# Bonus argument and bonus product of the scan conditions on GpSimd instead of VectorE

## The chip, the cores and the metric

The kernel runs on one core of one Trainium2 chip. The metric is device time in microseconds (us) of one execution; lower is better. Engines are called as in the profile: PE (matmul), PEld (its weight loads), DVE (VectorE), ACT (ScalarE), POOL (GpSimd), SP (the engine that issues most DMAs).

## What is computed

Two transformer layers on x of shape (4, 256, 256): batch 4, 256 tokens, width 256. Each layer is a condition, causal attention with 16 heads of 16, a second condition, and a feed-forward block (an fp8 linear in layer 0, a mixture of 32 experts with top 6 in layer 1). A condition is a bidirectional scan whose k and v are both the side input:

```python
def _bi_wkv(r, k, v, w, u, time_emb):
    tf = sigmoid(sum(time_emb, axis=-1))[:, None, None]
    decay = exp(-exp(w))[None, :] * (0.5 + 0.5 * tf[:, :, 0])
    ek = exp(minimum(k, 30.0)); ekv = ek * v
    # nf, df: forward scans of ekv and ek; nb, db: the backward scans
    euk = exp(minimum(u[None, None, :] + k, 30.0))     # the bonus
    num = nf + nb - ekv + euk * v
    den = df + db - ek + euk
    return sigmoid(r) * (num / maximum(den, 1e-8)) * (0.8 + 0.2 * tf)

x = x + attn0(cond(x, side, side, w0, u0, c))
x = x + ffn0(cond(x, side, side, w1, u1, c))
x = x + attn1(cond(x, side, side, w2, u2, c))
x = x + ffn1(cond(x, side, side, w3, u3, c))
```

There are 4 conditions of 4 batches each, so 16 pairs (condition i, batch b). Since k and v don't depend on x, num / den of a pair can be computed long before its r is known.

## The kernel before

Channels lie on the 128 partitions (NC = 2 chunks), tokens along the free axis. Every engine has its own hand-written program, ordered by semaphores alone; nothing is scheduled by a tool.

**Attention.** `attention(L)` runs for layers L = 0 and 1. It has 16 steps v = 4b + u (batch b, quad of heads u). In step v, PE has made the scores of v+1 (`scores`, L769 and the masks L751); DVE takes their row maxima out of PSUM with two reductions (`maxima`, L1219: first 128 columns by 4 heads, then 256 by 4); PE then makes the turned scores of step v (`turned_scores`, L782, L786, L751), which waits for the maxima of v+1; ACT takes their exponential (`exps`, L463); PE makes the scores of v+2 into the same PSUM tile S, which waits for that exponential; the maxima of v+2 follow. So one turn of the loop is DVE maxima, PE turned scores, ACT exponential, PE scores. Between them PE also does the projections (L701, L732), the output product (L744) and the product with the values (L821).

**Scan work in the gaps.** After the maxima of v+1, DVE's program has scan work of one pair n (`ratio_of` says which). Even u: `bonus_arg` (L1066, two instructions, min(side + u, 30) into eu[.., 1]), `scan_forward` and `scan_backward` of the denominator (L1075, L1078, L1087), `scale_o` of the attention, `denominator` (L1095, L1099). Odd u: in some steps `residual` (L1239), then both scans of the numerator, `numerator` (L1106 the bonus product eu[.., 1] = eu[.., 0] * side, L1110 its sum with the scans), `refine` (L1116, L1118) and either `gate` and `next_input` (L1132, L1141) or `make_ratio` (L1125). 7 pairs are done in attention(0) (v = 0 to 13) and 6 in attention(1) (v = 0 to 11); pairs n = 0, 1 and 9 are done outside of the loops.

**ACT.** In an even step ACT's program is: `spread_decay` (L424), `bonus_exp` (L432, two instructions, waits for `bonus_arg`), in most steps `totals_inverse` (L475, L477), `exps` (L463), and later `inverse` (L439, L441), which waits for `denominator`.

**POOL.** Memsets at the start, a `partition_all_reduce` of the weight maximum (L361) and, after attention(0), one of the input maximum (L365); then nothing until the indirect DMAs of the experts (L374), whose first one waits for step 12 of attention(1).

## Time and profile before

| | |
|---|---|
| median of 3 runs | 635.13 us (633.89 to 639.38) |
| the profiled execution | 637.68 us |
| its span, first to last instruction | 635.8 us |
| mean granted TensorE clock | 0.924 |
| DVE busy | 493.5 us, 78% |
| PE busy | 489.2 us, 77% |
| ACT busy | 336.2 us, 53% |
| POOL busy | 216.5 us, 34% |
| attention(0), attention(1) | about 47 to 163 us, 214 to 345 us |

Times in rows are counted from the first instruction. In a timeline a row is a start, a duration, the engine, the line of the kernel, the operation, what it writes <- reads, and how many instructions the row merges; a bracket at its end is the engine's idle time ahead of it and what ended that. Ends of matmuls are modelled.

### The profile page before, as it was taken

To read this page: it belongs to the slowest core of one execution; us is meant where nothing else is said; L and a number is where in the kernel's file an instruction comes from. 1 tells how busy PE (TensorE), PEld (TensorE's weight loads), DVE (VectorE), ACT (ScalarE), POOL (GpSimd) and SP (SyncE) were. 2 spreads that over 40 slices of the span, in tenths; PEclk is the share of its full clock that TensorE was granted. 3 is DMA by queue.
4 is the path that set the end of the run, shared out by engine and by line. 5 is a ranking of instruction groups with operands and counts; after the bars stand their busy time and mean duration, and the time that the engine had idled before them with its cause. 6 is when DMAs were issued, how large, how long until landed. Compare 5 with 4: busy or idle time off the path is not lost.

```text
span 635.8 us, 13234 instructions
## 1 busy us (share of the span) xinstructions
PE 489.2 (77%) x4916; PEld 402.2 (63%) x4916; DVE 493.5 (78%) x963; ACT 336.2 (53%) x663; POOL 216.5 (34%) x165
## 2 busy tenths in 40 slices
PE   0268889897725598898959659989999999999930
PEld 0147667675514376676746435589999999999930
DVE  2997999999475789999963680379999999999910
ACT  4334565655565155657532521257777777777720
POOL 3000000000000000000007277508888888888881
PEclk9977999999957699999968988999999999999985
DMA  8999910000000000000002173375997869779323
GB/s 296 282 240 234 249 34 3 1 2 2 2 2 0 0 2 1 3 3 2 1 2 104 31 276 113 125 258 161 244 232 195 227 173 247 203 192 253 37 27 66
DMA packets 56720, 71.89 MB, mean 113 GB/s; under 512 B 11777, under 2 KB 45036, under 8 KB 56544
## 3 DMA queue, kind: packets, MB, share of 16 engines
q1 hardware_dynamic: 40272, 57.35, 31.2%
q0 software_dynamic: 16400, 13.87, 11.0%
q8 instruction: 33, 0.54, 0.4%
q14 instruction: 15, 0.12, 0.1%
HBM read 42.09 MB, written 37.04 MB: 124 GB/s over the span
## 4 chain that ended last, share of the span: by engine, by line
DVE 51%; PE 28%; issue 12%; ACT 5%; DMA 2%; POOL 1%; DVEq 1%; POOLq 0%; SPq 0%; ACTq 0%
DVE negmax L1219 9%; PE S L751 4%; DVE both L1087 3%; DVE wgu_s L1477 3%; DVE fwd L1075 3%; PE S L782 3%; DVE xgT L1496 3%; PE PJ L701 3%; DVE sg L1505 3%; PE S L769 3%; PE S L940 3%; DVE ek L1502 3%; DVE hidden_s L1511 3%; DVE wgu_s L1479 2%; PE S L786 2%
## 5 line engine op out<-in xcount | busy, mean ns | idle before, releaser
L999 PE MATMUL S<-xgT,wgu_s 128*128 128x384 f32 x576 | 108.0, 340 | 8.2 <-DVE sg L1505 7.4
L374 POOL DMA_INDIRECT xe_rows<-x_tok,slot_i x48 | 47.7, 994 | 177.6 <-issue 165.8
L999 PEld LDWEIGHTS S<-xgT,wgu_s 128*128 128x128 f32 x576 | 98.8, 188 | 14.6 <-issue 14.6
L385 POOL DMA_INDIRECT out<-sig,y_token x48 | 81.1, 1690 | 36.9 <-ACT sig L655 22.1
L385 POOL DMA_INDIRECT odd_out<-sig,y_token x48 | 81.0, 1688 | 14.7 <-issue 14.4
L463 ACT ACTIVATE prob<-S 128x1536 f32<-128x1536 f32 x32 | 46.4, 1451 | 60.2 <-PE S L751 59.7
L1219 DVE TENSOR_REDUCE negmax<-S 128x4 f32<-128x512 f32 x64 | 58.2, 952 | 16.2 <-PE S L751 16.2
L782 PE MATMUL S<-q_sb,k_sb 32*128 32x128 f32 (+1 forms) x512 | 37.9, 368 | 29.1 <-DVE negmax L1219 29.1
L365 POOL PARTITION_ALL_REDUCE amax_x<-amax_x x1 | 0.4, 375 | 151.5 <-DVE amax_x L1209 151.5
L782 PEld LDWEIGHTS S<-q_sb,k_sb 32*128 32x128 f32 x512 | 24.6, 196 | 38.6 <-DVE negmax L1219 36.9
L1014 PE MATMUL PJ<-wd_s,hidden_s 128*128 128x256 f32 x320 | 43.3, 282 | 1.9 <-ACT sig L655 1.9
L1014 PEld LDWEIGHTS PJ<-wd_s,hidden_s 128*128 128x128 f32 x320 | 41.9, 189 | 2.0 <-issue 2.0
L751 PE MATMUL S<-causal_b,ident_b 128*128 128x128 bf16 x512 | 42.6, 230 | 0.0
L769 PE MATMUL S<-k_sb,q_sb 32*128 32x256 f32 (+1 forms) x512 | 33.2, 377 | 11.3 <-ACT q_sb L497 6.9
L751 PEld LDWEIGHTS S<-causal_b,ident_b 128*128 128x128 bf16 x512 | 31.0, 102 | 16.3 <-issue 12.9
L1075 DVE TENSOR_TENSOR_SCAN fwd<-decay_t,ek 128x512 f32<-128x512 f32 x32 | 38.9, 1215 | 2.9 <-ACT decay_t L424 2.8
L1087 DVE TENSOR_TENSOR_SCAN both<-decay_t,fwd 128x512 f32<-128x512 f32 x32 | 39.2, 1224 | 1.3 <-DVE fwd L1078 0.3
L432 ACT ACTIVATE eu<-eu,neg_ln_q 128x256 f32<-128x256 f32 x32 | 14.5, 499 | 48.5 <-DVE eu L1066 44.7
L1496 DVE TENSOR_TENSOR xgT<-TB,xgT 128x384 fp32r<-128x384 f32 x64 | 32.7, 552 | 2.4 <-ACT xgT L645 1.5
L786 PE MATMUL S<-neg_rows,pick 32*128 32x128 f32 (+1 forms) x512 | 34.5, 341 | 0.0
L663 ACT ACTIVATE hidden_s<-ek 128x384 fp32r<-128x384 f32 x32 | 16.7, 523 | 28.7 <-DVE ek L1502 26.1
L769 PEld LDWEIGHTS S<-k_sb,q_sb 32*128 32x128 f32 x512 | 18.9, 201 | 20.0 <-issue 17.4
(212 smaller groups left out, 1083.3 us busy)
## 6 DMA issues: line engine op xcount, KB each, us to landing
xe_rows<-x8m SPq DMA_DIRECT2D x4, 3468.0 KB, 38.7
ratio<-xe_rows SPq DMA_DIRECT2D x32, 433.5 KB, 3.7
ek<-in_wgu SPq DMA_DIRECT2D x32, 384.0 KB, 4.4
x8m<-in_wd SPq DMA_DIRECT2D x32, 256.0 KB, 4.9
x<-in_x SPq DMA_DIRECT2D x1, 1024.0 KB, 7.0
odd_out<-x8m SPq DMA_DIRECT2D x1, 1024.0 KB, 26.5
out<-side SPq DMA_DIRECT2D x8, 128.0 KB, 5.6
out<-odd_out POOLq DMA_DIRECT2D x1, 1024.0 KB, 8.0
```

The costliest lines, as they stand in the source:

```text
L374: eng.indirect_dma_start(xe_rows, bass.IndirectOffsetOnAxis(slot_i[:, t, k:k + 1], 0), x_tok[:, t, :], None, bounds_check=ROWS - 1, oob_is ...
L385: eng.indirect_dma_start((out, odd_out)[j % 2], bass.IndirectOffsetOnAxis(y_token[:, j, t:t + 1], 0), ye_sb[:, j % 2, t, :], None, bounds_ ...
L751: ins = eng.matmul(S[:, i, lo:lo + P], ident_b[:, :], causal_b[:, turned, :], start=False, stop=lo > 0, skip_group_check=True)
L769: eng.matmul(S[:, i, cols], q_sb[rows, b % 2, u, st * P:(st + 1) * P], k_sb[rows, b % 2, u // 2, 0:P * (st + 1)], start=st == 0, stop=Fals ...
L782: eng.matmul(S[:, i, cols], k_sb[rows, b % 2, u // 2, kt * P:(kt + 1) * P], q_sb[rows, b % 2, u, q_cols], start=kt == 0, stop=False, skip_ ...
L786: eng.matmul(S[:, i, cols], pick[rows, :], neg_rows[rows, v % 2, q_cols], start=False, stop=False, skip_group_check=True)
L999: ins = eng.matmul(S[:, m, 0:CAP], fast(wgu_s[:, j % 2, a, k, m * P:(m + 1) * P]), fast(xgT[:, j % 2, b, k, :]), start=n == 0, stop=n == N ...
L1014: ins = eng.matmul(dst, fast(hidden_s[:, j % 2, h, t * P:(t + 1) * P]), fast(wd_s[:, j % 2, a, part, :]), start=n == 0, stop=n == 4)
L1075: eng.tensor_tensor_scan(flat(fwd[:, kv, :, :]), decay_t[:, buf, 0:NC * T], ek_of(kv, b), 0.0, ALU.mult, ALU.add).then_inc(sem("forward"), 1)
L1087: eng.tensor_tensor_scan(flat(both[:, kv, :, :])[:, ::-1], decay_t[:, buf, NC * T:0:-1], flat(fwd[:, kv, :, :])[:, ::-1], 0.0, ALU.mult, A ...
L1219: ins = eng.tensor_reduce(negmax[:, v % 2, st, :, 0], S[:, :, cols], AX.X, ALU.max, negate=True)
L1496: eng.tensor_tensor(fast(xgT[:, j % 2, LO, k, :]), TB[:, k, 0:CAP], xgT[:, j % 2, HI, k, :], ALU.subtract)\
```

## The change

`bonus_arg` and the bonus product of the 13 pairs that are done inside `attention` leave DVE's program and are written on POOL, in `bonuses(L)`. Each waits for a new semaphore `max_half`, which DVE raises when the first of the two reductions of a step's maxima is done. The bonus product further waits for `bonus_exp`, as it did on DVE. `numerator` on DVE now begins with the wait for `bonus_made`. `bonuses(0)` stands on POOL between the two `partition_all_reduce`, `bonuses(1)` behind the second. The three pairs outside of the loops stay on DVE.

```diff
@@ POOL
             eng.partition_all_reduce(gmax[:, 1:2], amax_w[:, :], P, bass.bass_isa.ReduceOp.max)\
                .then_inc(sem("gmax_w"), 1)
 
+            def bonuses(L):
+                for b in range(B):
+                    for u in range(QUADS):
+                        v = b * QUADS + u
+                        ratio_now = ratio_of(L, b, u)
+                        if ratio_now:
+                            i, bb, n, buf = ratio_now
+                            eng.wait_ge(sem("max_half"), B * QUADS * L + v + 2)
+                            if u % 2 == 0:
+                                eng.wait_ge(sem("num_made"), n - 1)
+                                settle(eng, "pool")
+                                for c in range(NC):
+                                    ins = eng.tensor_scalar(eu[:, buf, 1, c, :], side[:, c, tok(bb)],
+                                                            vec[:, V_U + i * NC + c:V_U + i * NC + c + 1], 30.0,
+                                                            ALU.add, ALU.min)
+                                ins.then_inc(sem("bonus_arg"), 1)
+                            else:
+                                eng.wait_ge(sem("bonus_exp"), n + 1)
+                                settle(eng, "pool")
+                                eng.tensor_tensor(eu[:, buf, 1, :, :], eu[:, buf, 0, :, :], side[:, :, tok(bb)],
+                                                  ALU.mult).then_inc(sem("bonus_made"), 1)
+
+            bonuses(0)
             eng.wait_ge(sem("amax_x"), B)
             eng.partition_all_reduce(amax_x[:, 1, :], amax_x[:, 0, :], P, bass.bass_isa.ReduceOp.max)\
                .then_inc(sem("gmax_x"), 1)
+            bonuses(1)
@@ DVE, numerator
-            def numerator(b, n, buf):
+            def bonus(b, n, buf):
 
                 eng.wait_ge(sem("bonus_exp"), n + 1)
                 eng.tensor_tensor(eu[:, buf, 1, :, :], eu[:, buf, 0, :, :], side[:, :, tok(b)], ALU.mult)\
                    .then_inc(sem("bonus_made"), 1)
+
+            def numerator(b, n, buf):
+
                 eng.wait_ge(sem("bonus_made"), n + 1)
@@ DVE, maxima
                 for st, cols in HALVES:
+                    if st:
+                        ins.then_inc(sem("max_half"), 1)
                     ins = eng.tensor_reduce(negmax[:, v % 2, st, :, 0], S[:, :, cols], AX.X, ALU.max, negate=True)
@@ DVE, attention
                             i, bb, n, buf = ratio_now
-                            bonus_arg(i, bb, n, buf)
                             scan_forward(i, bb, n, buf, 0)
```

DVE's program in steps 2 and 3 of attention(0), from the maxima of step 3 to the product's place in step 3. Before:

```order
L1219 TENSOR_REDUCE negmax<-S 128x4 x2
L1066 TENSOR_SCALAR eu<-side,vec 128x256 x2
L1075 SCALAR_TENSOR_TENSOR fwd<-decay_t,ek 128x512
L1078 TENSOR_TENSOR fwd<-fwd,inv_q 128x2
L1087 SCALAR_TENSOR_TENSOR both<-decay_t,fwd 128x512
...
L1219 TENSOR_REDUCE negmax<-S 128x4 x2
L1075 SCALAR_TENSOR_TENSOR fwd<-decay_t,ek 128x512
L1078 TENSOR_TENSOR fwd<-fwd,inv_q 128x2
L1087 SCALAR_TENSOR_TENSOR both<-decay_t,fwd 128x512
L1106 TENSOR_TENSOR eu<-eu,side 128x512
L1110 TENSOR_TENSOR nd<-both,eu 128x512
```

The same place of the changed kernel (L1252 are the maxima, L1101 and L1113 the scans, L1139 the sum):

```order
L1252 TENSOR_REDUCE negmax<-S 128x4 x2
L1101 SCALAR_TENSOR_TENSOR fwd<-decay_t,ek 128x512
L1104 TENSOR_TENSOR fwd<-fwd,inv_q 128x2
L1113 SCALAR_TENSOR_TENSOR both<-decay_t,fwd 128x512
...
L1252 TENSOR_REDUCE negmax<-S 128x4 x2
L1101 SCALAR_TENSOR_TENSOR fwd<-decay_t,ek 128x512
L1104 TENSOR_TENSOR fwd<-fwd,inv_q 128x2
L1113 SCALAR_TENSOR_TENSOR both<-decay_t,fwd 128x512
L1139 TENSOR_TENSOR nd<-both,eu 128x512
```

The two `TENSOR_SCALAR` and the product are gone from DVE, and both times a scan now follows the maxima or the scans directly.

POOL's program from the first `partition_all_reduce` on (an `ISA` row without operands is an instruction that the toolchain put in: it sets which library of POOL's code is loaded; `ISA` with operands is the `partition_all_reduce`; a row's waits are all those since the row ahead of it). Before:

```order
L361 ISA
L361 ISA gmax<-amax_w 128x1 [waits amax_w]
L365 ISA amax_x<-amax_x 128x4 [waits amax_x]
L374 DMA xe_rows<-x_tok,slot_i 12288x289 [waits slots_made,x_tok_made,weights_made,slots_zeroed]
```

The changed kernel, the same start and then the stretch around the second `partition_all_reduce` (L390):

```order
L361 ISA
L361 ISA gmax<-amax_w 128x1 [waits amax_w]
L376 ISA [waits max_half,num_made]
L376 TENSOR_SCALAR eu<-side,vec 128x256 x2
L383 TENSOR_TENSOR eu<-eu,side 128x512 [waits max_half,bonus_exp]
...
L383 TENSOR_TENSOR eu<-eu,side 128x512 [waits max_half,bonus_exp]
L390 ISA
L390 ISA amax_x<-amax_x 128x4 [waits amax_x]
L376 ISA [waits max_half,num_made]
L376 TENSOR_SCALAR eu<-side,vec 128x256 x2
L383 TENSOR_TENSOR eu<-eu,side 128x512 [waits max_half,bonus_exp]
```

Where there was one `ISA` row without operands there are now four. The three new ones are in front of the first `TENSOR_SCALAR` of attention(0), in front of the second `partition_all_reduce`, and in front of the first `TENSOR_SCALAR` of attention(1). The first and the third of them stand behind the waits for `max_half` and `num_made`.

## Rows read from the trace of the kernel before

**Rows 1.** Table by stretch: us, then busy us (instructions) of each engine, clock.

```profile
47.00:163.00 116.00, 99.79 (x1506) 76.22 (x1508) 106.96 (x166) 65.63 (x116) 0.00 (x0) 0.97 0.32 73
214.00:345.00 131.00, 108.85 (x1538) 82.94 (x1538) 107.44 (x188) 64.07 (x116) 8.11 (x9) 0.91 0.03 10
```

**Rows 2.** Groups by shape, DVE: busy us, mean ns | idle us before, releaser.

```profile
L1219 DVE TENSOR_REDUCE negmax<-S 128x4 f32<-128x512 f32 x32 | 22.1, 689 | 16.2 <-PE S L751 16.2
```

**Rows 3.** Timeline, two steps of attention(0) in which DVE is late.

```profile
61.85 0.67 DVE L1106 TENSOR_TENSOR eu<-eu,side 128x512 f32<-128x512 f32 x1
62.55 0.69 DVE L1110 TENSOR_TENSOR nd<-both,eu 128x512 f32<-128x512 f32 x1
...
64.57 0.62 PE L751 MATMUL S<-causal_b,ident_b 128*128 128x128 bf16 x8
...
66.08 1.82 DVE L1219 TENSOR_REDUCE negmax<-S 128x4 f32<-128x512 f32 x2
67.81 0.60 DVE L1066 TENSOR_SCALAR eu<-side,vec 128x256 f32<-128x256 f32 x2
...
68.33 1.21 DVE L1075 TENSOR_TENSOR_SCAN fwd<-decay_t,ek 128x512 f32<-128x512 f32 x1
68.45 0.91 ACT L432 ACTIVATE eu<-eu,neg_ln_q 128x256 f32<-128x256 f32 x2 [3.01 <-DVE eu L1066]
...
69.66 0.42 ACT L477 ACTIVATE den_o<-den_o 128x256 f32<-128x256 f32 x1
...
70.13 1.45 ACT L463 ACTIVATE prob<-S 128x1536 f32<-128x1536 f32 x1
...
71.72 0.94 PE L769 MATMUL S<-k_sb,q_sb 32*128 32x128 f32 x16 [1.13 <-ACT prob L463]
...
72.59 0.62 PE L751 MATMUL S<-causal_b,ident_b 128*128 128x128 bf16 x8
...
73.40 1.81 DVE L1219 TENSOR_REDUCE negmax<-S 128x4 f32<-128x512 f32 x2
```

**Rows 4.** Timeline, a step of attention(0) in which DVE waits for PE.

```profile
88.99 0.62 PE L751 MATMUL S<-causal_b,ident_b 128*128 128x128 bf16 x8
...
89.64 1.82 DVE L1219 TENSOR_REDUCE negmax<-S 128x4 f32<-128x512 f32 x2 [0.29 <-PE S L751]
```

**Rows 5.** Timeline, the last step of attention(1) with a moved product.

```profile
317.57 0.62 PE L751 MATMUL S<-causal_b,ident_b 128*128 128x128 bf16 x8
...
323.24 1.82 DVE L1219 TENSOR_REDUCE negmax<-S 128x4 f32<-128x512 f32 x2
```

**Rows 6.** Groups by shape, POOL.

```profile
L345 POOL MEMSET negmax<- 128x512 f32 x1 | 0.5, 524 | 0.0
L356 POOL MEMSET inner<- 128x255 f32 x1 | 0.3, 324 | 0.0
```

**Rows 7.** Timeline, DVE and then POOL around the first `partition_all_reduce`.

```profile
29.63 0.68 DVE L1184 TENSOR_REDUCE amax_w<-w8raw 128x1 f32<-128x512 bf16 x1
30.41 0.46 POOL L361 PARTITION_ALL_REDUCE gmax<-amax_w  x1 [24.66 <-DVE amax_w L1184]
```

**Rows 8.** Instructions of L361: duration ns min/median/max, first and last start.

```profile
L361 POOLq MODIFY_POOL_CONFIG  x2: 25/25/25, 5.7 to 5.8; - x2
```

**Rows 9.** DMA issues: KB each, median us from issue to landing.

```profile
ident_b<-in_ident_b SPq DMA_DIRECT2D x1, 32.0 KB, 6.1
...
vec<-in_vec SPq DMA_DIRECT2D x1, 13.0 KB, 1.7
```

**Rows 10.** Timeline, step 0 of attention(0) and of attention(1).

```profile
47.34 1.83 DVE L1219 TENSOR_REDUCE negmax<-S 128x4 f32<-128x512 f32 x2 [0.72 <-PE S L751]
...
55.99 0.94 PE L769 MATMUL S<-k_sb,q_sb 32*128 32x128 f32 x16
...
220.38 1.82 DVE L1219 TENSOR_REDUCE negmax<-S 128x4 f32<-128x512 f32 x2 [3.88 <-PE S L751]
...
227.91 0.94 PE L769 MATMUL S<-k_sb,q_sb 32*128 32x128 f32 x16
```

More of the change, by code:

```diff
@@ L1175, in _ @@
             scan_backward(0, 0, 1)
+            bonus(0, 0, 0)
             numerator(0, 0, 0)
@@ L1196, in condition_input @@
                 scan_backward(n, buf, 1)
+                bonus(b, n, buf)
                 numerator(b, n, buf)
```

## Prediction, made before the changed kernel was run

> **What bounds the kernel now.** I read the table by stretch first: the change acts in the two attention stretches alone, and in both DVE is the busiest engine, 106.96 of 116 us and 107.44 of 131 us, with PE close behind at 99.79 and 108.85 [rows 1]. So DVE work taken away may count, but an average doesn't say in which steps. The groups by shape show that DVE waits ahead of its maxima for PE's masks for 16.2 us in all [rows 2]: there are steps in which PE is late instead.
>
> So I took the timeline step by step. The loop runs from the end of one step's maxima to the start of the next along two paths: DVE's scan work, and PE's turned scores, ACT's exponential, PE's next scores. Where DVE is late, the masks that end the scores are done well before the maxima start: in step 1 of attention(0) at 64.57 + 0.62 = 65.19, the maxima at 66.08, so 0.89 us; two rows later 72.59 + 0.62 = 73.21 against 73.40, so 0.19 [rows 3]. Where PE is late, the maxima follow the masks by 0.03 to 0.04 us (88.99 + 0.62 = 89.61, then 89.64), and DVE has even idled 0.29 us [rows 4]. The first number less 0.04 is what a step can gain at most. Read so for all 26 steps that carry a moved operation, from 47.34 [rows 10] to 323.24 [rows 5], 13 have something to gain, and in the other 13 PE is late:
> - odd steps, in which the product is moved and a scan follows the maxima at once: 0.85, 0.84, 0.59 (v = 1, 3, 13 of attention(0)), 0.85, 0.84 (v = 1, 3 of attention(1));
> - odd steps with `residual` ahead of the scan: 1.00, 0.76, 0.64, and 5.0 in the last [rows 5];
> - even steps, in which the argument is moved: 0.15, 0.24, 0.14, 0.83.
>
> **What the change takes away.** The two L1066 hold the next scan back from 67.81 to 68.33, 0.52 us; the product L1106 holds L1110 back from 61.85 to 62.55, 0.70 us [rows 3]. Times 13 pairs that is 15.9 us of DVE time. On the path it is the lesser of this and the step's number above: odd 7 x 0.70 + 0.59 + 0.64 = 6.13, even 0.15 + 0.24 + 0.14 + 0.52 = 1.05, together 7.2 us. The rest only makes DVE wait for PE longer.
>
> **What POOL costs.** The trace has no arithmetic on POOL. Its nearest rows are memsets: 524 ns for 512 columns and 324 for 255, so 0.1 us and 0.8 ns a column [rows 6]. A product of 512 columns reads two streams and writes one. It can't be cheaper than the memset, 0.52 us, and if its three streams pass one after the other it takes 1.37. I take 1.16, between two and three streams in turn, since nothing shows that reads overlap. The two argument instructions of 256 columns are 0.65 us together with one stream each and 1.06 with two; I take 0.85. POOL starts 0.69 us (first reduction [rows 2]) + 0.10 (from DVE's end at 30.31 to POOL's start at 30.41 [rows 7]) after the maxima's start. The arguments are then done at 0.79 + 0.85 = 1.64, and the product at 0.79 + 1.16 = 1.95. DVE used to go on at 67.81 - 66.08 = 1.73 and used to end the arguments at 2.33 [rows 3].
>
> Two things hang on these times. First, ACT: its `bonus_exp` stands in front of the step's exponential, and ACT came free at 69.66 + 0.42 = 70.08 for an exponential that started at 70.13 [rows 3]. There was no room, but with the arguments at 1.64 instead of 2.33 this path gets 0.7 us shorter, and is no concern below 1.54 us for the pair. Second, DVE: its scan reads two tensors of SBUF at 1.73 while POOL's product may still read two. No row has both engines at work there. The bounds are nothing and the whole rest of POOL's instruction, 1.95 - 1.73 = 0.22 us; I take the 0.22, since the two overlap in time. It counts in the five odd steps without `residual` (there 0.70 becomes 0.48): 5 x 0.48 + 3 x 0.70 + 0.64 + 1.05 = 6.2 us. For the even steps it is nothing.
>
> The Trainium skill, SBUF — State Buffer, "Which ops grab the shared pair", says that a DVE instruction with two SBUF inputs and a GpSimd instruction that reads SBUF exclude each other, the first one blocking the other until it has ended. By that rule the 0.22 is due in full and the gain is 6.2; by the idle POOL of rows 1 alone it would be 7.2. No run here shows it yet.
>
> **What the three new library rows cost.** The order shows `ISA` rows that switch POOL's library. The one at the first arguments of each attention stands behind the wait for `max_half`, so whatever it takes begins only then; behind it on POOL are the arguments, for which ACT's `bonus_exp` waits, and behind that the exponential of step 0, for which PE's scores of step 2 wait. The third, ahead of L390, stands behind the last product and is needed only when attention(0) is over, so it is hidden. POOL's indirect DMAs come after step 12 of attention(1), so none of them is held back.
>
> The price R of one switch isn't in the trace. Its two records take 25 ns each, at 5.7 us, and the reduction that needs the library runs at 30.41 [rows 7, 8]: R lies between 0.05 and 24.6 us. If code has to be fetched, the nearest rows are input DMAs: 1.7 us for 13 KB, 6.1 for 32 KB [rows 9]. I take 6.
>
> How much is hidden, in attention(0): first reduction and POOL's start 47.34 + 0.79 = 48.13; the arguments end at 48.98 + R; 0.04 and `bonus_exp` 0.91 [rows 3], 0.04, the exponential 1.45, and 0.14 to PE (71.58 to 71.72 [rows 3]): PE's scores of step 2 could start at 51.56 + R. They started at 55.99 [rows 10]. So 4.43 us of R are hidden and 1.57 show. In attention(1): 220.38 + 4.22 + R = 224.60 + R against 227.91 [rows 10]: 3.31 hidden, 2.69 show. Both together 4.26 us. DVE's denominator also waits for `bonus_exp`: in attention(0) it begins at 55.93 and takes about 0.69 + 0.60, as L1110 and L1066 do [rows 3], so it ends at 57.2, and the scores of step 2, started at 57.56, end behind that.
>
> The Trainium skill, GPSIMD Engine Reference, section 2.1, gives about 6 us (5.95) for the code load at the first call into a freshly loaded library, with no instruction visible for it. By the records' 25 ns the two switches would be free and the sum 6.2 us faster; by the page they take back 4.2 of it.
>
> **Sum.** -6.2 + 4.3 = -1.9 us. Against the profiled execution that is 637.68 - 1.9 = 635.8 (span 633.9). That execution lies 2.5 us above the median of 635.13; from the median I predict 633.2.
>
> **Rivals.**
> - *Forecast:* the switch takes 4 to 8 us. At 4 only 0.69 shows, 629.6; at 8 it is 3.57 + 4.69 = 8.3, 637.2. Chance 0.53.
> - *The switch is free or hidden:* library 0 may be what POOL held at the start, and switching back may need no fetch. For it: 25 ns records. Against it: the instructions stand right where they are needed. 635.13 - 6.2 = 628.9, and 627.9 if POOL and DVE don't hinder each other. Chance 0.20.
> - *The switch is long (ends on the other side):* at R = 10 it shows 5.57 + 6.69 = 12.3, so +6.1 and 641.2. It decides from 2R - 7.74 = 6.2, R = 7.0, on. For it: the only switch of before had 24.6 us of cover, so no row speaks against 10. PE's clock could add to it, since PE would then idle 7 us longer in attention(1), where the granted clock is 0.91 already. Chance 0.20.
> - *POOL's arithmetic is slow:* a product of 2.4 us ends at 3.19 and holds the scan for 1.46, 0.76 more than is saved, in 5 steps that DVE binds and about 0.7 in 4 where it is tied with PE; arguments of 1.7 us hold ACT by 0.16 in about 10 steps and DVE by 0.24 net in 4. That is 3.8 + 2.8 + 1.6 + 1.0 = 9 us in place of the gain, and with it 2 x 0.85 more of the switches shows, 4.3 + 1.7 = 6.0: 650. The product decides from 1.73 + 0.70 - 0.79 = 1.64 us on. Against it: memsets near 0.8 ns a column. Chance 0.07.
>
> **How the numbers follow.** 1% (6.35 us) is about what a measurement of this kernel can tell from no change. Below 628.8 lies a little over half of the second case, 0.12. Above 641.5 lie half of the long switch and most of slow arithmetic, 0.15. The rest, 0.73, is within 1%. The range 628.5 to 642 leaves out about 0.1 on each side; the likeliest case's own is 629.6 to 637.2.
>
> **What would show it.** POOL: the product at about 1.2 us, the arguments at 0.4 each; between DVE's first reduction of step 1 and the first argument a gap of R in each attention, 6 us, and nowhere else. PE's scores of step 2 late by 1.6 and 2.7 us against the maxima ahead. DVE: in steps v = 1 and 3 the scan 0.2 us later behind the maxima than 1.73; maxima in 12 or so of the 13 steps now waiting for PE or less late; idle ahead of L1252 above 16.2 us by some 14 (9.7 of the 15.9 that do not shorten the path, 4.3 of the switches). Attention(0) shorter by 1.7 us (3.2 gained, 1.6 given back), attention(1) by 0.3 (3.0 and 2.7). I am wrong if R is far from 6, if POOL's instructions pass 1.6 us, or if the maxima themselves get longer than 1.82 while POOL works.

## The result, and the profile after

The kernel became slower: 656.56 us median (655.56 to 659.55, 4 runs) against 636.38 (633.89 to 639.38) for the kernel before on the same chip, a ratio of 1.033 [1.029, 1.036]. I had predicted 633.2 and a range of 628.5 to 642. The profiled execution took 655.95 us, its span is 654.1 against 635.8.

The groups of instructions of the kernel after (line, engine, operation, tiles; busy us, mean ns; idle time of the engine just before them, and what ended it). Where a line moved: L1252 is L1219 of before, L1101 is L1075, L458 is L432, L489 is L463, L795 is L769.

```profile
L376 POOL TENSOR_SCALAR eu<-side,vec 128x256 f32<-128x256 f32 x26 | 35.8, 1378 | 146.5 <-DVE negmax L1252 75.6 <-issue 69.9
L383 POOL TENSOR_TENSOR eu<-eu,side 128x512 f32<-128x512 f32 x13 | 16.5, 1268 | 75.2 <-DVE negmax L1252 75.2
L458 ACT ACTIVATE eu<-eu,neg_ln_q 128x256 f32<-128x256 f32 x32 | 14.5, 500 | 76.2 <-POOL eu L376 64.1 <-DVE eu L1092 8.2 <-DVE den_cap L1197 3.8
L1252 DVE TENSOR_REDUCE negmax<-S 128x4 f32<-128x512 f32 x32 | 22.1, 691 | 18.4 <-PE S L777 18.2
L1101 DVE TENSOR_TENSOR_SCAN fwd<-decay_t,ek 128x512 f32<-128x512 f32 x32 | 41.5, 1298 | 3.9 <-ACT decay_t L450 3.9
```

The product takes 1.27 us, near the 1.16 assumed. The argument pair should have taken 0.85; each of its instructions takes 1.38 us on average. The third row points at the loss: ACT, which was to wait less, stands idle ahead of `bonus_exp` for 64.1 us because of GpSimd's arguments, in 12 places. In the kernel before it stood idle there for 44.7 us because of DVE's arguments, in 13.

The same two stretches as [rows 1], in the kernel after (busy us of each engine, number of instructions; granted clock as a share of full speed):

```profile
47.00:163.00 116.00, 95.70 (x1356) 71.69 (x1354) 93.35 (x134) 57.02 (x107) 27.27 (x20) 0.93 0.34 77
214.00:345.00 131.00, 102.78 (x1372) 77.81 (x1376) 105.20 (x169) 63.27 (x121) 23.75 (x18) 0.89 0.01 2
```

In the first stretch DVE's busy time falls from 106.96 to 93.35 us, and PE's from 99.79 to 95.70. PE lost no work, so in 116 us the kernel now gets less of the same work done, and a part of DVE's fall is that too. The load was taken off DVE, and no other engine filled the room.

An even step of the kernel after, its timeline (start, duration, engine, line, operation, tiles, idle before and its releaser). It is the step whose counterpart begins at 66.08 in [rows 3]:

```profile
71.72 1.82 DVE L1252 TENSOR_REDUCE negmax<-S 128x4 f32<-128x512 f32 x2 [0.27 <-PE S L777]
72.65 2.97 POOL L376 TENSOR_SCALAR eu<-side,vec 128x256 f32<-128x256 f32 x2 [7.45 <-DVE negmax L1252]
73.46 1.21 DVE L1101 TENSOR_TENSOR_SCAN fwd<-decay_t,ek 128x512 f32<-128x512 f32 x1
75.65 0.91 ACT L458 ACTIVATE eu<-eu,neg_ln_q 128x256 f32<-128x256 f32 x2 [3.71 <-POOL eu L376]
76.46 0.36 ACT L501 ACTIVATE den_o<-TB 128x256 f32<-128x256 f32 x1
76.85 0.42 ACT L503 ACTIVATE den_o<-den_o 128x256 f32<-128x256 f32 x1
77.18 1.43 ACT L489 ACTIVATE prob<-S 128x1536 f32<-128x1536 f32 x1
...
78.75 0.94 PE L795 MATMUL S<-k_sb,q_sb 32*128 32x128 f32 x16 [2.51 <-ACT prob L489]
...
80.51 1.82 DVE L1252 TENSOR_REDUCE negmax<-S 128x4 f32<-128x512 f32 x2 [0.62 <-PE S L777]
```

GpSimd starts 0.93 us into the maxima, but its pair ends at 75.62, 3.90 us in. Behind it stand `bonus_exp`, the two totals and the exponential, in this order on ACT, so the exponential starts 77.18 - 73.54 = 3.64 us behind the maxima; before it was 70.13 - 67.90 = 2.23 [rows 3]. PE then sits idle for 2.51 us for it, and the next maxima wait for PE.

Step 0 of attention(0), timeline, to be held against the first lines of [rows 10]:

```profile
47.26 1.82 DVE L1252 TENSOR_REDUCE negmax<-S 128x4 f32<-128x512 f32 x2 [0.72 <-PE S L777]
...
55.66 2.37 POOL L376 TENSOR_SCALAR eu<-side,vec 128x256 f32<-128x256 f32 x2 [24.88 <-issue]
58.07 0.91 ACT L458 ACTIVATE eu<-eu,neg_ln_q 128x256 f32<-128x256 f32 x2 [12.19 <-POOL eu L376]
58.88 1.43 ACT L489 ACTIVATE prob<-S 128x1536 f32<-128x1536 f32 x1
...
60.36 1.66 PE L795 MATMUL S<-k_sb,q_sb 32*128 32x128 f32 x16 [5.25 <-ACT prob L489]
...
63.02 1.82 DVE L1252 TENSOR_REDUCE negmax<-S 128x4 f32<-128x512 f32 x2 [2.61 <-PE S L777]
```

The records of the library switch among the instructions of L376 (ns of one, min/median/max, and the first and last start):

```profile
L376 POOLq MODIFY_POOL_CONFIG  x4: 11/11/11, 48.2 to 231.0; - x4
```

Two of them stand at 48.2, and the two of attention(1) at 230.6 and 231.0; the first arguments start at 55.66 and 237.98. From the first record to the argument it is 7.5 and 7.4 us: that is one switch. PE's scores of step 2 start at 60.36 in place of 55.99, and take 1.66 us in place of the 0.94 that the same sixteen take elsewhere.

**Where the 18.3 us of span lie.** I took the length from the end of a step's maxima to the next maxima, step by step in both traces, after minus before:

| steps | attention(0) | attention(1) | together |
|---|---|---|---|
| step 0 | +5.59 | +5.77 | +11.4 |
| even steps with an argument | +6.57 (6 steps) | +5.03 (5 steps) | +11.6 |
| odd steps with a product | -1.40 (7) | -1.33 (6) | -2.7 |
| between the attentions, and steps without moved work | | | -1.3 |

The sum is 19.0 at the last maxima; the stages behind take 0.7 us less than before. So three things have to be told apart: the switch, the arguments, and the product.

One entry belongs to none of them. Step 8 of attention(1) is 0.51 us longer, and it is so in every kernel of this document in which the product is on GpSimd, arguments moved or not (two of them, `e4_free_product` and `e5_early_free`, lose 0.9 us more there). The step ahead of it is 0.51 us shorter in all of them. The scan of step 8, first in the kernel before and then in the product-only kernel below:

```profile
288.12 1.22 DVE L1075 TENSOR_TENSOR_SCAN fwd<-decay_t,ek 128x512 f32<-128x512 f32 x1 [0.46 <-ACT decay_t L424]
```

```profile
284.69 1.23 DVE L1101 TENSOR_TENSOR_SCAN fwd<-decay_t,ek 128x512 f32<-128x512 f32 x1 [0.96 <-ACT decay_t L450]
```

DVE waits there for ACT's `decay_t`, which stands behind two `ACT_TABLE_LOAD` of 1.28 us each; ahead of these is a copy that waits for PE. What DVE gains in step 7 it loses again at this wait: 0.46 us becomes 0.96. So the arguments cost 11.1 us in ten steps, and the product gains 2.2 us net of this here.

### The profile page after: what moved, and what is told of

Its sections match the earlier page's. It is cut to its first block, busy times and chain, and to the rows that moved or that the text cites. A ratio compares the mean times of both kernels' runs of the same rounds, so it can differ in the third digit from the quotient of the medians.

```text
span 654.1 us, 13266 instructions
## 1 busy us (share of the span) xinstructions
PE 496.0 (76%) x4916; PEld 405.3 (62%) x4916; DVE 484.1 (74%) x924; ACT 333.4 (51%) x663; POOL 268.4 (41%) x204
## 4 chain that ended last, share of the span: by engine, by line
PE 25%; DVE 22%; issue 21%; POOL 19%; ACT 9%; DMA 1%; POOLq 1%; SPq 0%; DVEq 0%; ACTq 0%
POOL odd_out L411 7%; POOL out L411 7%; DVE negmax L1252 5%; POOL eu L376 5%; PE S L777 4%; PE S L795 4%; ACT prob L489 3%; PE S L966 3%; DVE both L1113 2%; DVE fwd L1101 2%; PE S L808 2%; PE PJ L727 2%; PE TB L983 2%; ACT eu L458 2%; PE S L812 1%
## 5 line engine op out<-in xcount | busy, mean ns | idle before, releaser
L376 POOL TENSOR_SCALAR eu<-side,vec 128x256 f32<-128x256 f32 x26 | 35.8, 1378 | 146.5 <-DVE negmax L1252 75.6
L489 ACT ACTIVATE prob<-S 128x1536 f32<-128x1536 f32 x32 | 46.2, 1443 | 60.6 <-PE S L777 60.6
L1252 DVE TENSOR_REDUCE negmax<-S 128x4 f32<-128x512 f32 x64 | 58.3, 953 | 18.4 <-PE S L777 18.2
L795 PE MATMUL S<-k_sb,q_sb 32*128 32x256 f32 (+1 forms) x512 | 34.5, 389 | 29.4 <-ACT prob L489 22.4
L458 ACT ACTIVATE eu<-eu,neg_ln_q 128x256 f32<-128x256 f32 x32 | 14.5, 500 | 76.2 <-POOL eu L376 64.1
L383 POOL TENSOR_TENSOR eu<-eu,side 128x512 f32<-128x512 f32 x13 | 16.5, 1268 | 75.2 <-DVE negmax L1252 75.2
L777 PE MATMUL S<-causal_b,ident_b 128*128 128x128 bf16 x512 | 44.6, 237 | 0.0
L1101 DVE TENSOR_TENSOR_SCAN fwd<-decay_t,ek 128x512 f32<-128x512 f32 x32 | 41.5, 1298 | 3.9 <-ACT decay_t L450 3.9
L795 PEld LDWEIGHTS S<-k_sb,q_sb 32*128 32x128 f32 x512 | 19.6, 207 | 38.6 <-issue 20.6
L777 PEld LDWEIGHTS S<-causal_b,ident_b 128*128 128x128 bf16 x512 | 32.5, 105 | 17.0 <-issue 13.5
L1113 DVE TENSOR_TENSOR_SCAN both<-decay_t,fwd 128x512 f32<-128x512 f32 x32 | 39.2, 1224 | 1.1
```

The costliest lines, as they stand in the source:

```text
L376: ins = eng.tensor_scalar(eu[:, buf, 1, c, :], side[:, c, tok(bb)], vec[:, V_U + i * NC + c:V_U + i * NC + c + 1], 30.0, ALU.add, ALU.min)
L489: eng.activation(prob[:, v % 2, :, :], S[:, :, 0:3 * P], ACT.Exp).then_inc(sem(f"exp_{L}"), 1)
L777: ins = eng.matmul(S[:, i, lo:lo + P], ident_b[:, :], causal_b[:, turned, :], start=False, stop=lo > 0, skip_group_check=True)
L795: eng.matmul(S[:, i, cols], q_sb[rows, b % 2, u, st * P:(st + 1) * P], k_sb[rows, b % 2, u // 2, 0:P * (st + 1)], start=st == 0, stop=Fals ...
L1101: eng.tensor_tensor_scan(flat(fwd[:, kv, :, :]), decay_t[:, buf, 0:NC * T], ek_of(kv, b), 0.0, ALU.mult, ALU.add).then_inc(sem("forward"), 1)
L1113: eng.tensor_tensor_scan(flat(both[:, kv, :, :])[:, ::-1], decay_t[:, buf, NC * T:0:-1], flat(fwd[:, kv, :, :])[:, ::-1], 0.0, ALU.mult, A ...
```

## The experiments

A word on comparing them: every ratio is to runs of the kernel before on the same chip. "The product-only kernel" below is `e2_product_only`.

### Holding the library ready

`e1_preload` adds one operation of a single column behind each all-reduce, so that the switch is made long before step 0:

```diff
+            def preload():
+                eng.wait_ge(sem("vec_in"), 16)
+                eng.tensor_scalar(tiny[:, :], vec[:, 0:1], 1.0, None, ALU.mult).then_inc(sem("settled_pool"), 1)
+
+            preload()
...
+            preload()
             bonuses(1)
```

> The changed kernel, with one tensor_scalar of a single column put on POOL right behind each partition_all_reduce, so that the library switch is made there and no longer behind the wait for max_half. Theory (three separate parts add up): step 0 of each attention loses what it got longer, 5.59 and 5.76 us, since 2.4 to 3.0 us of arguments alone let ACT's exponential start 3.1 us behind the maxima and PE needs it only at 4.1; the even steps keep their 0.8 to 1.9 us. About 645 us, ratio to before 1.014. Rival A (step 0 is long because POOL's first arithmetic is slow, not because of the switch): no more than 2 us faster than the changed kernel, 655. Rival B (switch and arguments overlap in some way that the sum does not show): between, 648 to 652.

Measured: 646.74 us, 1.016 [1.012, 1.020]. Step 0 is back at its old length (-0.53 and +0.02 us against before). The switch now stands where nothing waits (timeline of GpSimd in this kernel, behind the all-reduce that ends at 31.36):

```profile
38.57 0.71 POOL L367 TENSOR_SCALAR tiny<-vec 128x1 f32<-128x1 f32 x1 [7.21 <-issue]
48.76 2.96 POOL L383 TENSOR_SCALAR eu<-side,vec 128x256 f32<-128x256 f32 x2 [9.48 <-DVE negmax L1260]
```

GpSimd idles for 7.21 us with nothing to wait for: that is the switch. The same row in attention(1) shows 7.68. The measured time lies between the theory's 645 us and the lower end of rival B, 648, nearer the theory. Moved out of step 0 the switch gives back 1.65% of the time, about 10.5 us; the even steps keep their excess.

### The product alone

`e2_product_only` is `e1_preload` with the argument back on DVE:

```diff
-                            eng.wait_ge(sem("max_half"), B * QUADS * L + v + 2)
-                            if u % 2 == 0:
-                                eng.wait_ge(sem("num_made"), n - 1)
...
-                            else:
+                            if u % 2:
+                                eng.wait_ge(sem("max_half"), B * QUADS * L + v + 2)
...
                             i, bb, n, buf = ratio_now
+                            bonus_arg(i, bb, n, buf)
                             scan_forward(i, bb, n, buf, 0)
```

> As e1_preload, but the bonus argument is back on DVE: POOL makes the product alone. Theory (the arguments on POOL are the loss, the product is a gain): no exponential waits any longer; the product of 1.27 us holds the scan by 0.3 us, so an odd step that DVE bound gains 0.40, and those with the residual ahead 0.5 to 0.7: 5 x 0.4 + 2.7 = 4.7 us under before, about 631.7, ratio 0.993. Rival (POOL and DVE reading SBUF together costs DVE as much as it saves): 636 or more, ratio 1.000 or above, with scans above 1.5 us in even steps too.

Measured: 631.91 us, 0.994 [0.991, 0.998], a little faster than the kernel before, with the interval clear of 1, and faster than the changed kernel. Between `e1_preload` and this one only the argument moves: 2.2%, about 14 us, is its price. What is left, 0.6% or 3.6 us, is the product's gain; the interval allows 1.4 to 5.8. In its trace the gain is 0.21 or 0.22 us in each of the five odd steps where the scan follows the maxima and DVE is late, and 0.50 to 0.75 in four where `residual` stands ahead of it, 3.3 us together. Step 8 of attention(1) takes 0.51 of it back, so 2.8 us are left. The first of them, timeline of DVE and GpSimd in this kernel:

```profile
57.74 1.82 DVE L1252 TENSOR_REDUCE negmax<-S 128x4 f32<-128x512 f32 x2 [4.14 <-PE S L777]
58.64 1.27 POOL L382 TENSOR_TENSOR eu<-eu,side 128x512 f32<-128x512 f32 x1 [19.90 <-DVE negmax L1252]
59.48 1.51 DVE L1101 TENSOR_TENSOR_SCAN fwd<-decay_t,ek 128x512 f32<-128x512 f32 x1
...
61.22 1.22 DVE L1113 TENSOR_TENSOR_SCAN both<-decay_t,fwd 128x512 f32<-128x512 f32 x1
62.55 0.69 DVE L1139 TENSOR_TENSOR nd<-both,eu 128x512 f32<-128x512 f32 x1
```

and in the kernel before:

```profile
57.52 1.82 DVE L1219 TENSOR_REDUCE negmax<-S 128x4 f32<-128x512 f32 x2 [3.87 <-PE S L751]
59.26 1.21 DVE L1075 TENSOR_TENSOR_SCAN fwd<-decay_t,ek 128x512 f32<-128x512 f32 x1
...
60.71 1.23 DVE L1087 TENSOR_TENSOR_SCAN both<-decay_t,fwd 128x512 f32<-128x512 f32 x1
```

Two things are to be seen. The scan beside GpSimd's product takes 1.51 in place of 1.21 us. And the sum `nd` starts 62.55 - 62.44 = 0.11 us behind the second scan's end, where before it came 62.55 - 61.94 = 0.61 us behind it [rows 3]. The product had begun 0.09 us ahead of that scan's recorded end; with the product gone, the sum waits for the scan itself. So 0.50 is saved, not 0.70, and 0.50 - 0.30 = 0.20 is what the step shows.

### The argument one pair earlier

`e3_arg_early` keeps both operations on GpSimd and makes each argument in the even step before the one that uses it:

```diff
+                        if u % 2 == 0 and r + 1 < 2 * B and ratio_of(L, (r + 1) // 2, 2 * ((r + 1) % 2)):
+                            argument(L, r + 1, v)
                         ratio_now = ratio_of(L, b, u)
-                        if ratio_now:
+                        if ratio_now and u % 2:
```

> As e1_preload, but the argument of a pair is made on POOL one pair (two steps) earlier, at the same place within a step, so that ACT never waits for it while POOL's load and its overlap with DVE stay the same. Theory (the even steps got long because ACT's bonus_exp, and behind it the exponential, waited for POOL): the exponential starts 2.24 us behind the maxima again, the even steps go back to 5.50 to 5.88 or shorter, and the whole is at or below product only: about 630.7, ratio 0.991. Rival (they got long through the port that POOL and DVE share): they stay at 6.6 to 7.2 us and the whole stays near e1_preload, 645.

Measured: 634.06 us, 0.996 [0.993, 0.999]. GpSimd's pair runs at the same place of the step and is just as long, but nobody waits for it. Timeline of an even step of this kernel, DVE, GpSimd and ACT:

```profile
64.50 0.90 ACT L473 ACTIVATE eu<-eu,neg_ln_q 128x256 f32<-128x256 f32 x2
65.03 1.82 DVE L1267 TENSOR_REDUCE negmax<-S 128x4 f32<-128x512 f32 x2
...
65.94 2.97 POOL L378 TENSOR_SCALAR eu<-side,vec 128x256 f32<-128x256 f32 x2 [7.08 <-DVE negmax L1267]
...
69.08 1.45 ACT L504 ACTIVATE prob<-S 128x1536 f32<-128x1536 f32 x1 [2.38 <-PE S L792]
```

The exponential starts 69.08 - 66.85 = 2.23 us behind the maxima again, and the even steps have their old length. That tells the two explanations of the even steps apart: ACT's wait for a late argument made them long, not GpSimd's work beside DVE. The time was expected at or below the product-only kernel's, near 630.7, and came out 2 us above it, with intervals that overlap. In the trace, whose execution took 636.64 us, the excess lies in step 0 of attention(1), where the granted clock from 219 to 225 us is 0.50 (1.00 in the product-only kernel), in the stretch ahead of it, and in steps 12 and 13, which carry no moved work. What lowers the clock there is not shown. Of the other even steps three are 0.15 to 0.24 us shorter than in the product-only kernel, and none is longer.

### What an operation of GpSimd costs

`p2_probe_held` is the kernel before with nine probes on GpSimd at the start, DVE held until they are done (`p1_probe` is the same with DVE at work beside them; one execution each, 655.40 and 640.78 us):

```diff
+            step(eng.tensor_scalar(dst[:, 0:T], src[:, 0:T], 1.0, None, ALU.mult))
+            step(eng.tensor_scalar(dst[:, 0:T], src[:, 0:T], vec[:, V_U:V_U + 1], 30.0, ALU.add, ALU.min))
+            step(eng.tensor_scalar(dst[:, 0:T], src[:, 0:T], 2.0, 30.0, ALU.add, ALU.min))
...
+            step(eng.tensor_tensor(dst[:, :], src[:, :], hs[:, 2, :], ALU.mult))
+            step(eng.tensor_copy(dst[:, 0:T], src[:, 0:T]))
```

> The kernel of before with nine single POOL instructions put in front of the first partition_all_reduce, each waiting for the one ahead, on a scratch tile, while DVE has little to do: what POOL's arithmetic costs by itself. Theory A (a cost per column of tensor_scalar with two operations): 256 columns with pointer and immediate 1.14 us, 512 columns about 2.2, one operation clearly less. Theory B (the scalar read through a pointer is what costs): the forms with immediates near 0.35, those with a pointer 1.14. Theory C (a fixed cost of about 0.6 us for every tensor_scalar): 512 columns about 1.7. tensor_tensor of 512 columns 1.27, of 256 about 0.7, copy about 0.35 in all three. The time of the whole is within 1% of before.

> As p1_probe, but DVE's whole program first waits for the nine POOL instructions, so that nothing shares SBUF's engine side with POOL while they run; the whole gets longer by what DVE waits, some 15 to 20 us. In p1_probe DVE was busy beside them, and its times can't be told from waits. Theory A (tensor_scalar costs per column and per operation): 256 columns with two operations 1.14 with pointer or immediates alike, with one operation less, 512 columns about 2.1. Theory B (the pointer costs): immediates clearly shorter than pointers. Theory C (a fixed 0.6 us or more): 512 columns less than 1.6.

Timeline of GpSimd, kernel `p2_probe_held`, in the order of the probes:

```profile
17.51 0.89 POOL L371 TENSOR_SCALAR hs<-hs 128x256 f32<-128x256 f32 x1 [10.46 <-issue]
18.50 1.16 POOL L372 TENSOR_SCALAR hs<-hs,vec 128x256 f32<-128x256 f32 x1
19.75 1.06 POOL L373 TENSOR_SCALAR hs<-hs 128x256 f32<-128x256 f32 x1
20.91 0.93 POOL L374 TENSOR_SCALAR hs<-hs,vec 128x256 f32<-128x256 f32 x1
21.93 0.85 POOL L375 TENSOR_SCALAR hs<-hs 128x256 f32<-128x256 f32 x1
22.87 2.00 POOL L376 TENSOR_SCALAR hs<-hs,vec 128x512 f32<-128x512 f32 x1
24.95 0.72 POOL L377 TENSOR_TENSOR hs<-hs 128x256 f32<-128x256 f32 x1
25.75 1.26 POOL L378 TENSOR_TENSOR hs<-hs 128x512 f32<-128x512 f32 x1
27.08 0.40 POOL L379 COPY hs<-hs 128x256 f32<-128x256 f32 x1
```

With DVE quiet an argument of 256 columns costs 1.16 us, and one of 512 columns 2.00: 3.3 ns a column and 0.3 us fixed. A tensor by tensor product of the same 512 columns costs 1.26. So on GpSimd an operation with one input and two scalar operators is dearer than one with two inputs, and 2.9 times a copy (0.40). Most of that gap is there with a single operator already: 0.85 or 0.89 us, twice the copy. The second operator costs 0.2 us more (1.06 against 0.85), and a scalar read from SBUF through a pointer 0.1 us (0.93 against 0.85, 1.16 against 1.06). Of the three theories A fits best: the pointer matters least, against B, and 512 columns cost 2.00, against C. With DVE at work the probe of L372 took 2.14 us in place of 1.16.

### The product released earlier

Is the wait for the first maxima good for anything? `e4_free_product` is the product-only kernel with the product released by `bonus_exp` alone; `e5_early_free` does the same to `e3_arg_early`:

```diff
                             if u % 2:
-                                eng.wait_ge(sem("max_half"), B * QUADS * L + v + 2)
                                 eng.wait_ge(sem("bonus_exp"), n + 1)
```

> As e2_product_only, but the product no longer waits for max_half: it runs as soon as bonus_exp is done, in the even step, where DVE has scans and sums as well. Theory (the product's end overlaps the first scan of the odd step and lengthens it by 0.30 us; moved away, this is won back, and the even steps can bear a wait since PE binds most of them): first scans of the odd steps at 1.21 us, DVE-bound odd steps 6.23 us instead of 6.52, the whole 5 x 0.3 = 1.5 us under e2_product_only, about 630.4, ratio to before 0.992. Rival (the release at the half of the maxima is what keeps POOL out of DVE's way, and anywhere else the two block each other more): even steps above 5.9 us and the whole above e2_product_only, 633 or more.

> As e3_arg_early (arguments on POOL a pair ahead), with the product released by bonus_exp alone. Theory: adds 0.5 to 1.0 us in the DVE-bound even steps to e4_free_product: about 629.8, ratio 0.991. Rival (POOL now has the argument and the product in the same even step, 2.97 + 1.27 us of the 7.7, and DVE's scans and sums wait for it): even steps above 6.2 us, 635 or more.

Measured: 641.79 us, 1.008 [1.005, 1.011], and 638.7, 1.003 [1.001, 1.006]. My theory missed in both; for `e4_free_product` its rival holds. Timeline of an even step of `e4_free_product`:

```profile
68.10 1.22 DVE L1100 TENSOR_TENSOR_SCAN fwd<-decay_t,ek 128x512 f32<-128x512 f32 x1
68.22 0.91 ACT L457 ACTIVATE eu<-eu,neg_ln_q 128x256 f32<-128x256 f32 x2 [2.50 <-DVE eu L1091]
...
69.31 1.27 POOL L381 TENSOR_TENSOR eu<-eu,side 128x512 f32<-128x512 f32 x1 [17.17 <-ACT eu L457]
69.36 1.25 DVE L1103 TENSOR_TENSOR fwd<-fwd,inv_q 128x2 f32<-128x2 f32 x1
...
70.64 1.23 DVE L1112 TENSOR_TENSOR_SCAN both<-decay_t,fwd 128x512 f32<-128x512 f32 x1
```

DVE's tiny product of two columns, 0.16 us elsewhere, takes 1.25: it starts 0.05 us after GpSimd's product and ends 0.03 after it. Against the product-only kernel ten even steps get 0.70 to 1.09 us longer; five odd ones gain the 0.30 that the scan no longer loses. The scan of 1.51 us shows the same from its side: by the records GpSimd's product runs 0.43 us into it (58.64 + 1.27 = 59.91 against 59.48), and it is 0.30 longer. Where a DVE instruction with two SBUF inputs meets GpSimd's product, it ends only behind it; the maxima, which read PSUM, take 1.82 us beside GpSimd as without it. The release at the first maxima is what makes the two meet for 0.43 us and not for all 1.27. The Trainium skill, SBUF — State Buffer, "Who interferes with whom", states that a DVE instruction with two SBUF inputs and a GpSimd instruction that reads SBUF exclude each other, the second one standing still until the first has ended. For the product these runs agree: 1.09 us more for 1.22 us of overlap, 0.30 for 0.43. For the arguments they agree only one way: a GpSimd argument that starts while a scan runs gets 0.62 us longer, but the scan at 73.46 in the changed kernel starts 0.33 us before GpSimd's first argument ends, and takes 1.21 us as ever.

`e5_early_free` is another matter. In its trace the even steps are not above 6.2 us, as the rival had it, but for steps 0, 8 and 10 of attention(1), which are above it in the kernel before too. Steps 2 are 0.3 us longer than in `e3_arg_early`, step 8 of attention(1) 0.9, and the last maxima come 3.8 us earlier than there. The time is lost behind them, where nothing was changed, 4.2 us against `e3_arg_early`, most of it in the first 34 us, where the granted clock is 0.87 against 0.95. So its time doesn't show what the early product costs there.

### The switch alone

`e6_switch_only` was to put the switch alone into step 0, behind the wait for `max_half`, with the arguments on DVE and `bonus_exp` of that step waiting for the one-column operation:

```diff
+            def preload(L):
                 eng.wait_ge(sem("vec_in"), 16)
+                eng.wait_ge(sem("max_half"), B * QUADS * L + 2)
                 eng.tensor_scalar(tiny[:, :], vec[:, 0:1], 1.0, None, ALU.mult).then_inc(sem("settled_pool"), 1)
```

> As e2_product_only (arguments on DVE), but the library switch stands behind the wait for max_half in step 0 of each attention, with a tensor_scalar of one column behind it for which ACT's bonus_exp of that step waits: the switch on the path without the slow arguments. Theory (a switch of about 7.2 us, of which step 0 hides 4.4 and 3.3): the exponential of step 0 starts at 47.3 + 0.9 + 7.2 + 0.7 + 1.0 = 57.1, so PE's scores are 2.5 us late in attention(0) and 4 to 5 in attention(1), and PE's clock falls to its lower level once more, 1 us or more each: 8 to 10 us above e2_product_only, 640 to 642, ratio 1.007 to 1.010. Rival (the two arguments, not the switch, carry most of the 11.4 us of the two steps): under 4 us above e2_product_only, 636 or less.

Measured: 632.59 us, 0.992 [0.990, 0.995], far from it. The edit had not done what it was meant to: the program's order has the library's `ISA` row ahead of the wait, so that the switch was made early once more. Its records stand at 30.8 us, right behind the first all-reduce, and the one-column operation starts at 48.22 us, right at its release, and takes 0.27. It says nothing on the price in step 0, but it is a second kernel like the product-only one, and as fast. `e7_switch_held` puts an event between the wait and the operation, and the switch then stands behind the wait, its records at 48.2 us:

```diff
                 eng.wait_ge(sem("max_half"), B * QUADS * L + 2)
+                settle(eng, "pool")
                 eng.tensor_scalar(tiny[:, :], vec[:, 0:1], 1.0, None, ALU.mult).then_inc(sem("settled_pool"), 1)
```

> Product on GpSimd, arguments on DVE, and in step 0 of each attention the library switch truly behind the wait for `max_half`: an event stands between the wait and the one-column operation, so the `ISA` row comes behind the wait; `bonus_exp` of step 0 waits for that operation. Theory (a switch takes 7.0 to 7.4 us from its wait on, and in step 0 part of it shows): the column starts 7.0 to 7.4 us after the first reduction's end, near 55.4; `bonus_exp` then starts near 55.8 in place of 49.8 and the exponential of step 0 near 56.7 in place of 53.2, so 3.5 us more in attention(0) and about as much in attention(1), 7 us together and up to 1.5 more from TensorE's clock. Against the 632.6 (0.992) of the same kernel with the switch made early: 639 to 641, ratio 1.004 to 1.008. Rival (what made step 0 late was the arguments' own time, the switch being fetched beside other work): below 635, ratio 0.998 or less.

Measured: 639.59 us, 1.004 [1.001, 1.007], as expected. Timeline of step 0 of this kernel:

```profile
47.25 1.82 DVE L1254 TENSOR_REDUCE negmax<-S 128x4 f32<-128x512 f32 x2 [0.72 <-PE S L779]
...
55.76 0.26 POOL L369 TENSOR_SCALAR tiny<-vec 128x1 f32<-128x1 f32 x1 [24.99 <-issue]
56.05 0.91 ACT L458 ACTIVATE eu<-eu,neg_ln_q 128x256 f32<-128x256 f32 x2 [10.19 <-POOL tiny L369]
56.87 1.43 ACT L489 ACTIVATE prob<-S 128x1536 f32<-128x1536 f32 x1
...
58.35 1.55 PE L797 MATMUL S<-k_sb,q_sb 32*128 32x128 f32 x16 [2.01 <-ACT prob L489]
```

Step 0 is 3.47 us longer in attention(0) and 2.98 in attention(1) than in the kernel before. The switches alone cost 6.5 us there, some 7 us of the whole. Of the 6.5 us 5.4 are PE's scores starting late (2.45 and 2.98), and 1.0 is the scores and masks of attention(0), which take 1.55 and 1.03 us in place of 0.94 and 0.62.

### Half of the argument

`e8_half_argument` moves only the first of an argument's two tiles:

```diff
+                            eng.wait_ge(sem("max_half"), B * QUADS * L + v + 2)
+                            if u % 2 == 0:
+                                eng.wait_ge(sem("num_made"), n - 1)
+                                settle(eng, "pool")
+                                eng.tensor_scalar(eu[:, buf, 1, 0, :], side[:, 0, tok(bb)],
...
-                            bonus_arg(i, bb, n, buf)
+                            bonus_arg(i, bb, n, buf, (1,))
```

> Product on GpSimd with the library held ready, and of the argument only the first of its two tiles on GpSimd, the second left on DVE. Theory (ACT's wait is what costs, and GpSimd's work does not by itself hold DVE in an even step): the tile is done about 0.79 + 0.1 + 1.14 = 2.0 to 2.1 us after the maxima's start, as late as DVE's own tile, so the exponential starts 2.24 us behind the maxima as before, even steps are as long as in the product-only kernel or up to 0.26 shorter where DVE is late (4 steps), and the time is 631 to 632.5, ratio 0.991 to 0.995. Rival (DVE's own argument or its scan waits for GpSimd to finish, or GpSimd's tile is stretched as the second of a pair was, 1.76 us): the exponential starts 2.5 us or later behind the maxima, even steps 0.3 to 0.8 longer, 635 or more, ratio 0.998 or more.

Measured: 634.09 us, 0.996 [0.993, 0.999]. The trace decides for the theory, step by step: the exponential starts as far behind the maxima as in the product-only kernel in every even step, to 0.01 us (2.23 or 2.24 us in nearly all), three steps in which DVE was late are 0.14 to 0.15 us shorter than in the product-only kernel, and none is longer by more than 0.02. One tile of 1.15 us (mean of 13) is done before ACT needs it; two are not. The time missed the 631 to 632.5 expected, and is no better than the product-only kernel's: 0.5 us shorter by the last maxima, and 2.5 us longer behind them, where nothing was changed. The two intervals overlap, so neither version can be called the faster.

## Why the prediction was wrong

**What bounds the kernel: right but for one step.** In steps that DVE binds, moved work shortens the step, and where PE is late it does nothing; the product-only kernel and `e8_half_argument` show it step by step, outside of step 0 and of the steps without moved work. Overlooked was ACT's `decay_t` in step 8 of attention(1). The prediction counted 0.64 us for the product of step 7 and 0.52 for the argument of step 8 there, since DVE's maxima come late behind PE's masks. But DVE itself waits 0.46 us for ACT in that step, so the first was won and lost again, and the second could not be won.

**The step that failed first: the price of the arguments.** I took 0.85 us for the pair, from the memsets of [rows 6], and gave 1.06 as the upper end. It is 2.37 with DVE quiet (step 0), 2.97 in ten other steps, and 2.35 in step 8 of attention(1), where the scan starts only behind it. The rows could not carry this estimate: a memset has no operator and reads nothing, and the probes show that scalar operators cost more on GpSimd than a second input. For 256 columns a memset is 0.32 us, this operation 1.16. In the second place, the other 0.60 is DVE's: with the scan of L1101 beside it the pair's second instruction takes up to 1.76 us instead of 1.14. Step 8, without that overlap, is the counter-check. I had looked at the collision only from DVE's side, and only in odd steps.

**The threshold was right, and it condemned the change.** The prediction held ACT's path to be no concern below 1.54 us for the pair. At 2.97 it is 1.43 beyond, GpSimd starts another 0.14 later than assumed (0.93 us into the maxima, not 0.79), and the exponential comes 3.64 - 2.23 = 1.41 late. In three steps this costs 1.46 to 1.89 us; in six, in which PE has a projection to do ahead of its scores, 0.76 to 0.86; in step 10 of attention(1) 1.24; 11.1 us in ten steps. `e1_preload` against the product-only kernel gives 14 us for the argument. 1.4 us more of it is step 0 of attention(1), shorter in the product-only kernel, where the granted clock from 219 to 225 us is 1.00 (0.50 in the kernel before). In the traces of these two kernels another 1.5 us lies in steps 12 and 13 of attention(1), which carry no moved work; its cause is not shown. The rival with slow arithmetic (arguments of 1.7 us, 650 us) had this mechanism, but put 6.6 us of its cost on a product of 2.4 us, which was not slow. I gave it 0.07, since a row of 0.8 ns a column seemed to speak against it.

**The switch: right mechanism, and the 6 us assumed were too little.** One takes 7.0 to 7.7 us. By the working's own formula 7.5 and 7.4 show 7.5 - 4.43 = 3.1 and 7.4 - 3.31 = 4.1, 7.2 together. `e7_switch_held` shows 6.5, with an operation of 0.26 us where the formula has a pair of 0.85, and with slower matmuls in it. At 7.2 the switches outweigh the 6.2 of gain that was forecast: they are past the point of 7.0 from which, by the prediction, the time goes up. The Trainium skill, GPSIMD Engine Reference, section 2.1, gives about 6 us for a first call into a freshly loaded library; here the way back to plain tensor operations took at least 7.0.

**The two add up in step 0.** Switch, argument pair and `bonus_exp` stand one behind the other there, so that the 2.37 - 0.85 = 1.52 us too much for the pair shows in full, twice: 7.2 + 3.0 = 10.2. PE's scores start 4.45 and 5.46 us later behind the maxima than before, 9.9 together, and the two steps are 11.4 us longer. Most of the rest is PE in attention(0): after standing still for 5.25 us its sixteen scores took 1.66 us instead of 0.94 and the masks 1.03 instead of 0.62. In attention(1), after 4.24 us, the scores took 0.94 as before and only the masks were longer, 0.92. The granted clock shows it. The window 59:65, first in the kernel after, then in the one before (the last three columns are clock, DMA share, GB/s):

```profile
59.00:65.00 6.00, 4.64 (x48) 2.90 (x52) 3.29 (x6) 4.55 (x8) 1.07 (x1) 0.53 1.09 237
```

```profile
59.00:65.00 6.00, 5.60 (x76) 4.62 (x76) 5.75 (x9) 2.92 (x6) 0.00 (x0) 1.00 1.09 247
```

At 0.53 PE is close to the lower level of 1.2 GHz; in attention(0) the stall is paid once in waiting and again in slower matmuls. Around the stall of 2.51 us in the even step above, from 77 to 83 us, the granted clock is 0.74, against 1.00 before.

**The product: right in kind, its gain put too large.** 1.27 us against 1.16 assumed, 0.30 us of hold against 0.22. The saving of 0.70 was 0.50, since the product had covered the wait for the scan ahead of it. Five steps of 0.48 became 0.21 or 0.22, and the four behind `residual`, 2.74 together, 2.27; the gain was 3.3 us by these steps of the trace, 2.8 with step 8 of attention(1), against 5.1 in the working. In the even steps the forecast had 1.05 us for the argument. They could not come while ACT was late; `e8_half_argument` gets 0.43 of them with half of the argument.

**In sum,** the product gained some 3 us (2.8 by the steps, 3.6 by the times), the arguments lost 11 to 14, the switches 7 to 10, against 6.2 gained and 4.3 lost in the forecast. The range was too narrow because its upper end rested on one unknown, the switch, while the unknown price of the arithmetic was held to within 25% by a row of another kind of operation. That two costs stand one behind the other in step 0 was seen, but only with both at their cheap values.

## What to carry to other kernels

Before work is moved to an engine that has none of its kind in the trace, measure that operation in its own form (operators, inputs, size) by a probe beside the kernel: a memset says little about it. Ask first who waits for the moved result, and how late it may be: here the same GpSimd work cost 11 to 14 us where ACT waited for it, and no loss could be measured where it was made a pair earlier (0.996 of the time before, against 0.994 with the product alone). And look for what a moved operation brings with it: a library switch took 7.0 to 7.7 us, and cost nothing visible where it was called early, by an operation of one column behind the last use of the other library.

## What the hardware showed that I had not expected

- On GpSimd a `tensor_scalar` with two operators on 128x256 f32 took 1.16 us, with one 0.85 to 0.93, a `tensor_tensor` 0.72, a copy 0.40.
- GpSimd's product held a DVE product of two columns for 1.09 us, and a DVE scan with two SBUF inputs held GpSimd's `tensor_scalar` for 0.6. A GpSimd `tensor_scalar` already running did not hold the scan: 0.33 us of overlap, and 1.21 us as ever. Neither touched the maxima, which read PSUM.
- The library switch left two records of 11 ns (82 or 83 ns in `e1_preload` and `e6_switch_only`), and 7.0 to 7.7 us in which GpSimd stood idle with nothing to wait for. The other way, from tensor operations to the reduction's library, it was 6.50 us in `p1_probe`.
- A wait written ahead of an operation doesn't hold the switch that belongs to it: only with an event between the two did it start behind the wait (`e6_switch_only`, `e7_switch_held`), 7 us apart in time.
